# Expert layers of a four-layer network: the down-projection three tiles behind the transposes, with four buffers of split operands

## The reference

```python
# layers 0, 1, 3: E = 16, 8, 16 experts, hidden width F = 512; layer 2: 8 experts and a shared one, F = 1024
top2, idx = top_k(softmax_or_logits(xf @ gate_w + gate_b), 2)      # two experts for each token
h = act(xf @ w1[e] + b1[e])          # relu (layer 0), gelu (1, 2)
h = silu(xf @ w1[e]) * (xf @ w2[e])  # layer 3: two up-projections, no biases
y = h @ w_down[e] + b2[e]
x = x + sum over the two experts of weight * y    # layer 0 normalises once more
```

## Time and profile before

| What | us |
|---|---|
| Median of 3 runs | 1201.09 (1198.06 to 1204.16) |
| The profiled execution, its own time | 1190.06 |
| Its span, first to last instruction | 1188.3 |
| Busy in the span: PE, DVE, ACT, POOL | 951.9, 737.2, 504.8, 468.1 |
| Mean granted TensorE clock | 0.891 of full speed |

### The profile page before, as it was taken

The page is one execution under the profiler, slowest core; times in us unless marked ns, Lnnn a source line. Parts: engine busy times, 40 slices in busy tenths (PEclk is TensorE's granted clock), DMA queues, the critical chain, the costliest instruction groups (busy, mean ns, idle before and its releaser), DMA issues. The chain is left out here.

```text
span 1188.3 us, 23797 instructions
## 1 busy us (share of the span) xinstructions
PE 951.9 (80%) x7426; PEld 885.7 (75%) x7426; DVE 737.2 (62%) x1699; ACT 504.8 (42%) x933; POOL 468.1 (39%) x480
## 2 busy tenths in 40 slices
PE   5784978528888859856995999999628995899993
PEld 1684878525888859855895999999625885899993
DVE  4586655475777757647555656665454786666664
ACT  2151656310555617631102777776413451343441
POOL 1052565211867626530132355554103452345441
PEclk9695999869879969997997999999859997899997
DMA  6005965410000053744124051119440003846853
GB/s 231 1 23 174 299 222 175 123 41 0 6 10 10 10 182 99 229 137 130 54 67 177 29 196 35 37 47 334 175 128 2 6 14 114 312 162 206 278 186 125
DMA packets 65388, 142.22 MB, mean 120 GB/s; under 512 B 11008, under 2 KB 42656, under 8 KB 60320
## 3 DMA queue, kind: packets, MB, share of 16 engines
q1 hardware_dynamic: 55520, 114.52, 28.3%
q0 software_dynamic: 9792, 26.75, 7.5%
HBM read 219.36 MB, written 18.61 MB: 200 GB/s over the span
## 5 line engine op out<-in xcount | busy, mean ns | idle before, releaser
L1602 PE MATMUL r_pH<-e_xsT,e_w 128*128 128x128 f32 x2560 | 309.0, 278 | 25.5 <-DMA e_w<-w_in 20.6
L1602 PEld LDWEIGHTS r_pH<-e_xsT,e_w 128*128 128x128 f32 x2560 | 298.4, 194 | 29.5 <-issue 22.5
L1551 POOL DMA_INDIRECT y_rows<-e_ys,e_to x102 | 166.5, 1632 | 259.6 <-DVE e_idx L1670 122.2
L1682 DVE TENSOR_TENSOR e_w_lo<-e_w,e_w_hi 128x1024 fp32r<-128x1024 f32 (+1 forms) x102 | 156.2, 1532 | 45.8 <-ACT e_w_hi L1638 45.1
L1615 PE MATMUL r_pY<-e_w_hi,e_h_hi 128*128 128x256 f32 x528 | 159.1, 301 | 7.4 <-issue 5.8
L1638 ACT ACTIVATE e_w_hi<-e_w 128x1024 fp32r<-128x1024 f32 (+1 forms) x102 | 132.3, 1297 | 70.3 <-DMA e_w<-w_in 70.2
L1687 DVE TENSOR_TENSOR e_h_lo<-xnT,e_h_hi 128x512 fp32r<-128x512 f32 (+1 forms) x102 | 86.6, 849 | 119.8 <-ACT e_h_hi L1654 119.8
L1615 PE MATMUL r_pY<-e_w_lo,e_h_hi 128*128 128x256 f32 x528 | 150.4, 285 | 0.0
L1615 PE MATMUL r_pY<-e_w_hi,e_h_lo 128*128 128x256 f32 x528 | 150.4, 285 | 0.0
L448 PE MATMUL g_o<-g_V,g_pT 128*128 128x65 f32 (+2 forms) x896 | 145.0, 319 | 4.8 <-ACT g_pT L407 4.8
L1650 ACT ACTIVATE xnT<-r_pH,e_w 128x128 f32<-128x128 f32 x416 | 115.5, 377 | 71.3 <-PE r_pH L1602 71.1
(11 more groups left out here) (275 smaller groups left out, 1412.9 us busy)
## 6 DMA issues: line engine op xcount, KB each, us to landing
e_w<-w_in SPq DMA_DIRECT2D x64, 1024.0 KB
e_w<-w_in SPq DMA_DIRECT2D x84, 512.0 KB
e_w<-w_in SPq DMA_DIRECT2D x32, 1028.0 KB
e_w<-w_in SPq DMA_DIRECT2D x52, 514.0 KB
e_b<-b_in SPq DMA_DIRECT2D x84, 128.0 KB
e_w<-y_rows SPq DMA_DIRECT2D x24, 256.0 KB, 5.0
p_adj<-adj_in SPq DMA_DIRECT2D x8, 512.0 KB, 7.4
xn_rows<-xn SPq DMA_DIRECT2D x32, 128.0 KB, 1.7
```

The lines of the kernel that those rows point to most:

```text
L1551: pool.indirect_dma_start(out=y_rows[:, :], in_=ys[b][:, :], in_offset=None, out_offset=bass.IndirectOffsetOnAxis(ap=to[b][:, :], axis=0))\
L1602: ins = nc.tensor.matmul(pH[b % 2][:, f, :], w1[b][:, at:at + P], xsT[b % 2][:, c, :], start=(c == 0), stop=(c == DC - 1))
L1682: nc.vector.tensor_tensor(w2_lo[b % 2][:, :], w2[b][:, :], w2_hi[b % 2][:, :].bitcast(F32), ALU.subtract).then_inc(w2_split, 1)
```

## The change

In layers with `UN` of 4 (0, 1 and 3) three things change. Layer 2 keeps its code in effect.

1. The down-projection of a tile and its `end` come three steps behind its transpose and no longer two (`DEEP` = 3).
2. `h_hi`, `h_lo`, `w2_hi` and `w2_lo` have four buffers each and no longer two (`KEPT` = 4).
3. ACT rounds w2(s) after it has rounded h(s), no longer before it takes h(s). DVE splits w2 one step later: split_w2(s-2) stands where split_w2(s-1) stood.

The order at step s is then:

- PE: turn(s), rise(s-1), fall(s-3)
- ACT: function of h(s), round h(s), round w2(s)
- DVE: copy(s), split_w2(s-2), [product(s-1)], split_h(s-1), end(s-3)
- POOL and SP: as before

```diff
+                DEEP, KEPT = (3, 4) if UN == 4 else (2, 2)
-                h_hi, h_lo = ([ph.sb(f"{k}{n}", [P, FC, P], F32R) for n in range(2)] for k in ("h_hi", "h_lo"))
-                w2_hi, w2_lo = ([ph.sb(f"{k}{n}", [P, FC * D], F32R) for n in range(2)] for k in ("w2_hi", "w2_lo"))
+                h_hi, h_lo = ([ph.sb(f"{k}{n}", [P, FC, P], F32R) for n in range(KEPT)] for k in ("h_hi", "h_lo"))
+                w2_hi, w2_lo = ([ph.sb(f"{k}{n}", [P, FC * D], F32R) for n in range(KEPT)] for k in ("w2_hi", "w2_lo"))
...
-                        if not early(i, b, 2):
-                            fall(*before(i, b, 2))
+                        if not early(i, b, DEEP):
+                            fall(*before(i, b, DEEP))
                     gate_tensor(pe)
                     last = loop(pe, step)
                     rise(last, UN - 1)
-                    fall(last, UN - 2)
-                    fall(last, UN - 1)
+                    for n in range(UN - DEEP, UN):
+                        fall(last, n)
...
+                    def round_w2(i, b):
+                        t = UN * i + b
+                        act.wait_ge(w2_loaded[b], 16 * (i + 2))
+                        if not early(i, b, KEPT):
+                            act.wait_ge(y_summed, t - KEPT + 1)
+                        nc.scalar.activation(w2_hi[b % KEPT][:, :], w2[b][:, :], ACT.Copy).then_inc(w2_rounded, 1)
...
-                        act.wait_ge(w2_loaded[b], 16 * (i + 2))
-                        if not early(i, b, 2):
-                            act.wait_ge(y_summed, t - 1)
-                        nc.scalar.activation(w2_hi[b % 2][:, :], w2[b][:, :], ACT.Copy).then_inc(w2_rounded, 1)
+                        if KEPT == 2:
+                            round_w2(i, b)
                         act.wait_ge(h_summed, t + 1)
...
-                        nc.scalar.activation(h_hi[b % 2][:, :, :], hT[b % 2], ACT.Copy).then_inc(h_rounded, 1)
+                        if KEPT == 4 and not early(i, b, KEPT):
+                            act.wait_ge(y_summed, t - KEPT + 1)
+                        nc.scalar.activation(h_hi[b % KEPT][:, :, :], hT[b % 2], ACT.Copy).then_inc(h_rounded, 1)
+                        if KEPT == 4:
+                            round_w2(i, b)
...
                         copy(i, b)
+                        if not early(i, b, DEEP - 1):
+                            split_w2(*before(i, b, DEEP - 1))
                         if not early(i, b, 1):
-                            split_w2(*before(i, b, 1))
                             if kind == "silu":
                                 product(*before(i, b, 1))
                             split_h(*before(i, b, 1))
-                        if not early(i, b, 2):
-                            end(*before(i, b, 2))
+                        if not early(i, b, DEEP):
+                            end(*before(i, b, DEEP))
...
                     last = loop(dve, step)
-                    split_w2(last, UN - 1)
+                    if DEEP == 3:
+                        split_w2(last, UN - 2)
+                    else:
+                        split_w2(last, UN - 1)
                     if kind == "silu":
                         product(last, UN - 1)
                     split_h(last, UN - 1)
-                    end(last, UN - 2)
-                    end(last, UN - 1)
+                    end(last, UN - DEEP)
+                    if DEEP == 3:
+                        split_w2(last, UN - 1)
+                    for n in range(UN - DEEP + 1, UN):
+                        end(last, n)
```

More of the change, by code:

```diff
@@ L1611, in fall @@
                             pe.wait_ge(y_ready, t - 1)
-                        m = b % 2
+                        m = b % KEPT
                         for f in range(FC):
                             for n, (h, w) in enumerate(((h_hi, w2_hi), (h_hi, w2_lo), (h_lo, w2_hi))):
-                                ins = nc.tensor.matmul(pY[m][:, :], h[m][:, f, :], w[m][:, f * D:(f + 1) * D],
+                                ins = nc.tensor.matmul(pY[b % 2][:, :], h[m][:, f, :], w[m][:, f * D:(f + 1) * D],
                                                        start=(f == 0 and n == 0), stop=(f == FC - 1 and n == 2))
@@ L1681, in split_w2 @@
                         dve.wait_ge(w2_rounded, UN * i + b + 1)
-                        nc.vector.tensor_tensor(w2_lo[b % 2][:, :], w2[b][:, :], w2_hi[b % 2][:, :].bitcast(F32),
+                        nc.vector.tensor_tensor(w2_lo[b % KEPT][:, :], w2[b][:, :], w2_hi[b % KEPT][:, :].bitcast(F32),
                                                 ALU.subtract).then_inc(w2_split, 1)
@@ L1686, in split_h @@
                         dve.wait_ge(h_rounded, UN * i + b + 1)
-                        nc.vector.tensor_tensor(h_lo[b % 2][:, :, :], hT[b % 2], h_hi[b % 2][:, :, :].bitcast(F32),
+                        nc.vector.tensor_tensor(h_lo[b % KEPT][:, :, :], hT[b % 2], h_hi[b % KEPT][:, :, :].bitcast(F32),
                                                 ALU.subtract).then_inc(h_split, 1)
```

## The result

The changed kernel takes 1204.57 us (median of 20 runs, 1201.06 to 1223.11), the kernel before 1198.53 us (median of 20). The ratio is 1.005, with a 95% interval of 1.0034 to 1.0067: 6.0 us, 0.5%, slower. The forecast was +6.8 us and 1207.9.

A forecast was written before the change was run, and what follows sets the result against it. SP's queue was taken to bound layers 0 and 1, PE layer 3. Filling (1.9 + 1.4) and drains (2 x 1.65 + 0.2) made 6.8 us, added to a median of 1201.09: 1207.9 us, range 1198 to 1216.

The forecast's parts named there:

- the forecast's own range: Whole kernel: 1204 to 1211 us for the main forecast, which had a chance of 0.45.
- a sign of being wrong: New profile: PE waiting at transposes for `e_xs` would mean that gathers bind, as in rival 2.
- What bounds the kernel: SP's queue of register loads, branches and three issues a tile paces layers 0 and 1; PE bounds layer 3.
- Drains: Layer ends: last w2 split after h delays the last fall 1.65 us in layers 0 and 1, 0.2 in layer 3.
- Filling: Layer starts: w2(4) leaves SP 1.9 us later in layer 1, 1.4 in layer 0, delaying later loads; 3.3 us.
- POOL: Store waits a step longer, gather behind it: 4.0 to 4.2 us a tile, faster than SP's 4.96; costed at nothing.
- my threshold of 5.6: Gathers in layers 0 and 1 were to cost something only when they take over 5.6 us.
- rival 2: POOL's gathers become the bound in layers 0 and 1: 15 us more, 1216, or something between, 1212; chance 0.17.
- The steady steps: Middle of the layers: later w2_split waits on SP and ACT's h(t) ahead of w2 change nothing; costed at nothing.
- rival 3: Faster: ACT makes h without waiting for w2, so SP's w1 goes sooner; up to 11.4 us less, 1196.5; chance 0.12.

The follow-up runs named there:

- Run 11: Kernel before without the b2 reload for every tile in layers 0 and 1, the guessed expert's bias added; 1169.73 us, ratio 0.9743 to before.
- run 6: Changed kernel with stores six tiles behind the gathers and tile 0's w2 rounded and split early, as before the change; 1197.27 us, ratio 1.0037 to before.
- runs 7 and 8: 7: run 6 with b2 loads three tiles behind w1, 1201.80 us, ratio 1.0009; 8: run 3 with the same, 1202.54 us, ratio 1.0026.
- Run 1: Changed kernel with POOL's stores six tiles behind the gathers, not five, in the four-lane layers; 1199.99 us, ratio 1.0004 to before.
- run 5: Kernel before with stores six tiles behind the gathers, not five, in layers 0, 1 and 3; 1189.13 against 1190.49 us, ratio 0.9979.
- run 3: Changed kernel with w2 rounded first and split one step behind, and stores six tiles behind the gathers; 1206.52 us, ratio 1.0045 to before.
- runs 9 and 10: 9: changed kernel, SP waiting for w2_split before w1, 1205.77 us, ratio 1.0107; 10: run 2 with w2 held back in layer 3, 1201.51 us, ratio 1.0085.
- run 2: Changed kernel with w2 rounded ahead of h and split one step behind, as in the kernel before; 1210.80 us, ratio 1.008 to before.
- runs 7, 8, 11 and 12: One timing group, the kernel before at 1199.9 us; 12 is the changed kernel without b2 reloads in layers 0 and 1, 1196.79 us, ratio 0.9964.

## Why the prediction was right, and where it was not

The time, the sign and the size came out: 6.0 us against 6.8, inside the forecast's own range. The sum did not hold term by term, and that it came out is in part luck. The prediction had also named as a sign of being wrong that PE waits at transposes for `e_xs`, and it does, for 19.1 us.

- *What bounds the kernel*: right. Run 11 shows what SP's queue does for b2 to be worth 30 us, so that queue bounds layers 0 and 1. I had expected 12 to 18 there, because I took PE's waits for weights (20.6 us) for all that SP costs.
- *Drains*: right. 1.5 us in each of layers 0 and 1, for the reason given. In layer 3, the last rise comes about as much earlier as the drain is longer: run 6, with one gather wait of 1.3 us there, needs 156.3 us from the layer's first matmul on slots (line 1240) to its last fall; before needed 156.2. The changed kernel's own trace needs 159.6, and 1.1 us of that comes before the first rise.
- *Filling*: w2(4) was late by 1.84 us in layer 1, as forecast, but in layer 0 by 0.3 and not 1.4, and undoing it brings nothing (run 6). The step saw one wait of SP's queue and not the b2 load, whose `y_ready` is a step later too. Taken together the filling is worth 0 to 3 us (runs 7 and 8), not a certain 3.3.
- *POOL*: this is the step that failed. The chain was worked out right (12.0 us for three tiles), and then costed at nothing, because from rise(5) to rise(17) PE needs 4.49 us a tile on average. An average was the wrong thing to compare with. It is made of stretches at 3.42, while SP has no real loads to send, and of stretches at 5 and more. In the first the chain binds at once: gathers 6, 7 and 8 of layer 1 were taken by PE 2.9, 3.8 and 4.5 us after their issue, below my threshold of 5.6, and PE waited 0.4 to 0.5 us for each. PE is then late when it comes to the slow stretches, where some of it is taken back. Run 1 prices this at 5.5 us; the same edit gives the kernel before 1.4 to 2.5 (by the medians and by the ratio of run 5), which may be nothing. It is rival 2's mechanism, without its size (8 us and more on top).
- *The steady steps*, costed at nothing: here too something seems to be missing, the other way. Run 1 is 5 us faster than run 3, which has w2 first, but runs 7 and 8 show only 2 us of that, within their uncertainty. The direction is rival 3's, its mechanism is not seen: SP's pace stays at 4.89 us a tile and its w1 does not go out earlier. I had looked at one place in layer 1, where SP came 2.3 us after h, and did not read ACT's waits. Those of the kernel before, in layer 0:

```profile
ACT e_w_hi L1638 <- DMA e_w<-w_in: 27.2, 9, 6.5
```

In the changed kernel this row is gone. What that is worth is not shown.

Put together: the gathers (5.5 us), two drains (3.0) and the filling (0 to 3) make 8.5 to 11.5 us, and 6.0 were measured. So by this estimate some 2.5 to 5.5 us come back from something that the prediction had at nothing; given the intervals it may be less. The order of w2 is the candidate, and it is not proven. A missed loss and what looks like a missed gain cancelled for the most part, and the forecast was near for a reason that it did not have.

On POOL's durations: the stores beside DVE's two-input subtraction took 1.59 to 1.61 us here too. In the trace of the kernel before, the 19 stores that met no DVE operation took 0.96 to 0.99 us, some 50 that ran beside 0.7 to 0.8 us of the split of w2 took 1.6, and the 20 of layer 2, beside 1.7 to 1.8 us of a split twice as long, 2.6 to 2.7. Three stores met 0.8 to 1.0 us of a split and still took 1.0. So the longer time that the prediction used is what the stores take here; no run moves the split away from them to prove that it is the cause.

## What to carry to other kernels

A slack has to be read tile by tile: a chain that is slower than the engine in the fast stretches costs time even where it is faster than the average. When a pipeline is made a tile deeper, follow every signal that its last stage gives (here `y_ready`: the store, the gather queued behind it, the b2 load) and move each follower by the same tile. Before tuning the order on the engines, take the suspected queue out once: leaving one small load out of SP's queue was worth five times what this change moves. And before an experiment is read, look in its trace whether the edit did what it was for: two of mine (runs 9 and 10) did not.

## What had not been expected of the hardware

A queue that only issues can be the bound of two layers: three issues a tile with their register loads took SP 4.9 us, and without the b2 load the kernel was 30 us faster, although that load moves only 128 KB. Gathers of the same size landed 2.6 us after their issue at the least, and one in run 2 was taken by PE only after 8.2 us. And the executions of the kernel before spread from 1195.5 to 1206.8 us in one group with no change of code, more than the whole effect; a single trace is no measure of it. The granted clock goes with that spread: beside runs 7, 8, 11 and 12 the fastest execution of the kernel before, 1195.32 us, had a mean of 0.894, and the slowest, 1209.58 us, 0.881.
